# Splitting VectorE's copy of the gates' input parts in a two-group recurrence

## The reference

```
xi, xg, xo = xt @ U_i + b_i, xt @ U_c + b_c, xt @ U_o + b_o
def step(carry, xs):
    h, c = carry
    i_t = sigmoid(xi_t + h @ V_i)
    g_t = tanh(xg_t + h @ V_c)
    o_t = sigmoid(xo_t + h @ V_o)
    c_new = h * c + i_t * g_t
    h_new = o_t * tanh(c_new)
    return (h_new, c_new), h_new
```

## Time and profile before

| | |
|---|---|
| median of 3 runs | 3816.36 us (3816.0 to 3819.65) |
| the profiled execution | 3818.34 us, span 3816.5 us |
| busy share of the span | PE 92%, PEld 77%, DVE 76%, ACT 64%, POOL 34% |
| granted clock of TensorE, mean | 0.978 |
| VectorE copies into psGI (L2147) | 192, median 684 ns |
| GpSimd hc (L2205) | 192, mean 735 ns |

### The profile page before, as it was taken

How to read it: one execution, slowest core, us unless ns; L and a number is a source line. 1 busy time by engine, 2 the same in 40 slices (tenths; PEclk the granted TensorE clock), 3 DMA queues, 4 the chain that set the end, 5 groups by cost and what they waited for, 6 DMA issues and landing times. The chain is left out here.

```text
span 3816.5 us, 81795 instructions
## 1 busy us (share of the span) xinstructions
PE 3493.4 (92%) x30707; PEld 2953.6 (77%) x30707; DVE 2918.6 (76%) x4371; ACT 2444.4 (64%) x6220; POOL 1309.3 (34%) x735
## 2 busy tenths in 40 slices
PE   8878888888879988999999989999999979899987
PEld 7755555555559977888888878888888878788886
DVE  4679999999968865777777766777777767677887
ACT  4548888888855545666666655666666633677775
POOL 0009999999955541000000001000000024222254
PEclk9989999999989989999999999999999989999999
DMA  5674111211124321000000010000000046555575
GB/s 147 196 207 108 44 39 44 64 41 44 39 69 135 118 93 46 18 18 17 18 18 12 12 53 17 18 18 17 18 18 12 12 153 211 170 144 143 143 227 166
DMA packets 199348, 294.39 MB, mean 77 GB/s; under 512 B 17920, under 2 KB 155520, under 8 KB 195968
## 3 DMA queue, kind: packets, MB, share of 16 engines
q1 hardware_dynamic: 189824, 282.08, 24.7%
q10 hardware_dynamic: 9216, 8.39, 0.6%
HBM read 197.87 MB, written 92.54 MB: 76 GB/s over the span
## 5 line engine op out<-in xcount | busy, mean ns | idle before, releaser
L737 POOL TENSOR_TENSOR mx_big<-mp_lvs,mx_big 128x1280 f32<-128x1280 f32 (+1 forms) x224 | 709.9, 3239 | 282.3 <-ACT mp_lvs L657 277.5
L712 DVE TENSOR_TENSOR mx_big<-mp_psL,mx_big 128x2816 f32<-128x2816 f32 (+1 forms) x224 | 691.4, 3145 | 21.2 <-PE mp_psO L602 18.3
L664 ACT ACTIVATE mp_cut<-mp_psO,mx_mask 128x128 f32<-128x128 f32 x2048 | 553.1, 405 | 140.1 <-PE mp_psO L602 110.2
L602 PE MATMUL mp_psO<-mx_big,mp_pair 128*16 128x256 f32 x8192 | 498.5, 383 | 110.8 <-DVE mx_big L712 84.9
L1538 PE MATMUL sv_psO<-at_v_hi,sv_p_hi 128*128 128x258 f32 x2048 | 584.0, 285 | 13.5 <-DVE sv_p_lo L1626 10.3
L1557 ACT ACTIVATE sv_S<-sv_psS,at_kb 128x512 f32<-128x512 f32 x512 | 353.0, 689 | 372.1 <-PE sv_psS L1512 294.3
L1538 PE MATMUL sv_psO<-at_v_lo,sv_p_hi 128*128 128x258 f32 x2048 | 578.6, 282 | 0.0
L1538 PE MATMUL sv_psO<-at_v_hi,sv_p_lo 128*128 128x258 f32 x2048 | 577.7, 282 | 0.0
L1601 DVE TENSOR_TENSOR sv_run<-sv_run,sv_S 128x512 f32<-128x512 f32 x448 | 313.3, 699 | 289.2 <-ACT sv_S L1557 289.2
L602 PEld LDWEIGHTS mp_psO<-mx_big,mp_pair 128*16 128x16 f32 x8192 | 324.7, 127 | 249.2 <-DVE mx_big L712 136.9
L1538 PEld LDWEIGHTS sv_psO<-at_v_hi,sv_p_hi 128*128 128x128 f32 x2048 | 386.2, 189 | 43.1 <-DVE sv_p_lo L1626 21.1
(11 more groups left out here) (288 smaller groups left out, 7724.1 us busy)
## 6 DMA issues: line engine op xcount, KB each, us to landing
re_xg<-xg SPq DMA_DIRECT2D x192, 384.0 KB, 3.3
xg<-ga_xg SPq DMA_DIRECT2D x32, 768.0 KB, 4.0
att<-mx_big SPq DMA_DIRECT2D x16, 1024.0 KB, 6.7
mp_pair<-att SPq DMA_DIRECT2D x128, 128.0 KB, 2.9
mx_big<-rv SPq DMA_DIRECT2D x14, 1024.0 KB, 11.9
fr_xr<-in_x SPq DMA_DIRECT2D x16, 512.0 KB, 4.7
fr_xl<-in_x SPq DMA_DIRECT2D x32, 256.0 KB, 4.2
rv<-fr_rvs SPq DMA_DIRECT2D x16, 512.0 KB, 3.2
```

What stands on the lines that cost most here:

```text
L602: mm = pe.matmul(psO[32 * j:32 * j + 2 * H, c % 2, q, :], pair[:, s, :, :, c * YC + y], Z[:, c % 2, y, :], start=True, stop=True, tile_pos ...
L664: ins = nc.scalar.activation(cut[:, s, c, :, h * DK:(h + 1) * DK], psO[:, c % 2, :, h * DK:(h + 1) * DK], ACT.Copy, scale=mask[:, h:h + 1])
L712: nc.vector.tensor_tensor(Z[:, c % 2, 0:m], psL[:, s, 0:D].unsqueeze(1).broadcast_to([P, m, D]), rv_place(big, seventh, b, c)[:, 0:m], ALU ...
L737: nc.gpsimd.tensor_tensor(Z[:, c % 2, m:YC], lvs[:, s, :].unsqueeze(1).broadcast_to([P, YC - m, D]), rv_place(big, seventh, b, c)[:, m:YC] ...
```

## The change

The copy is made in two halves of 256 columns, each with its own semaphore. The half for gate g stays where the copy was, behind c and ahead of the wait for tanh. The half for gate i is made later in the same slot, behind ig and ahead of `keep_lo`. TensorE waits for the second half only before its matmuls on gate i; SyncE waits for both before it reloads the buffer. The first steps' copies, before the slots, are made in two halves one behind the other.

```diff
-        per_group = ("gi_filled o_filled ...
+        per_group = ("g_filled i_filled o_filled ...
@@ SyncE
-                            sp.wait_ge(q[g]["gi_filled"], r.nth(i - S) + 1)
+                            sp.wait_ge(q[g]["g_filled"], r.nth(i - S) + 1)
+                            sp.wait_ge(q[g]["i_filled"], r.nth(i - S) + 1)
@@ TensorE
                         pe.wait_ge(q[g]["hi_ready"], n + 1)
-                        pe.wait_ge(q[g]["gi_filled"], n + 1)
+                        pe.wait_ge(q[g]["g_filled"], n + 1)
                         terms(g, psGI[g][:, 1, 0:D], G_, HI)
+                        pe.wait_ge(q[g]["i_filled"], n + 1)
                         terms(g, psGI[g][:, 0, 0:D], I_, HI)
@@ VectorE, in cell
                         if i + 1 < r.steps:
-                            fill_gi(g, i + 1)
+                            fill_g(g, i + 1)
                         dve.wait_ge(q[g]["tanh_ready"], n + 1)
@@
-                    def fill_gi(g, i):
+                    def fill_g(g, i):
                         dve.wait_ge(xg_in[g][i % S], r.load(i))
                         reach(dve, q[g]["g_ready"], r.nth(i))
+                        nc.vector.tensor_copy(psGI[g][:, 1, 0:D], xg[:, g, i % S, G_]).then_inc(q[g]["g_filled"], 1)
+
+                    def fill_i(g, i):
                         reach(dve, q[g]["i_ready"], r.nth(i))
-                        gates = xg[:, g, i % S].rearrange("p (j d) -> p j d", j=3)
-                        nc.vector.tensor_copy(psGI[g][:, :, 0:D], gates[:, 0:2]).then_inc(q[g]["gi_filled"], 1)
+                        nc.vector.tensor_copy(psGI[g][:, 0, 0:D], xg[:, g, i % S, I_]).then_inc(q[g]["i_filled"], 1)
@@
                     for g in range(B):
-                        fill_gi(g, 0)
+                        fill_g(g, 0)
+                        fill_i(g, 0)
@@ VectorE, the slots
                         nc.vector.tensor_tensor(ig[:, g], gate[:, g, I_], gate[:, g, G_], ALU.mult).then_inc(q[g]["ig_ready"], 1)
+                        if 0 <= m < r.steps - 1:
+                            fill_i(o, m + 1)
                         if k < r.steps:
                             keep_lo(o, k)
```

More of the change, by code:

```diff
@@ L1925, in recurrent_steps @@
         outed = [[sem(f"outed{g}{s}") for s in range(S)] for g in range(B)]
-        per_group = ("gi_filled o_filled turned moved hi_ready lo_ready g_made i_made o_made g_ready i_ready o_ready ig_ready c_ready "
+        per_group = ("g_filled i_filled o_filled turned moved hi_ready lo_ready g_made i_made o_made g_ready i_ready o_ready ig_ready c_ready "
                      "tanh_ready h_ready hc_ready os_ready").split()
```

## The result

The changed kernel takes 3850.5 us (median of 4 runs) against 3816.2 us before: ratio 1.009, 95% interval 1.0076 to 1.0104. It is 34 us slower, as forecast (3851, with 34.0 us in the sum). The profiled execution took 3849.08 us, with a span of 3847.3 us.

A forecast was written before the change was run, and what follows sets the result against it. It took VectorE's own queue order (h_lo of one group, then c of the other) to bound the kernel at 2.77 us a slot. Terms 28.2 + 5.8 gave +34.0 us, so 3851 us, range 3824 to 3866.

The forecast's parts named there:

- (b) to (d): VectorE, fill_i between ig and h_lo: 0.33 us, slots of 2.99; +28.2 us in the first 128, +5.8 in the last 64.
- The price of the half: VectorE's 256-column copy behind ig: taken as 0.33 us a slot, between bounds of 0.20 and 0.60.
- The sum: Whole recurrence: 28.2 + 5.8 = +34.0 us.
- Part (a): Copy between c and h shrinks to 256 columns, so h waits only for tanh: gain 0.03 us a slot.
- What bounds the kernel before: Recurrence slot: a loop closed once a slot on VectorE's queue order, h_lo of one group, then c of the other: 2.77 us.
- The link from h to the cast: From h through the transposes to the cast at +1.08, which ends at +1.47 and releases h_lo at +1.50.
- The page's chain through TensorE: Profile page's chain, mostly through TensorE: not followed, because TensorE sits idle twice in every slot, once for 0.24 us.
- rival C: VectorE: fill_i fits before the cast, only the 0.03 gain is left: -6 us, 3810; chance 0.04.
- rival A: VectorE: ig is not really held by hc, only slowed by chance: total +7 us, 3823; chance 0.06.
- B: Last 64 slots: fill_i too is held by GpSimd, at the residual add: total +69 us, 3885; chance 0.08.
- Part (e): New waits, TensorE for the I half before its fifth gate matmul and SyncE's one more per load: costed at nothing.
- the cover: TensorE's margin from fill_i's end at +1.84 to its fifth gate matmul at +2.09: 0.25 us.

The follow-up runs named there:

- experiment 7: Changed kernel with a second copy of the same 256 columns ahead of fill_i, behind ig, into unused columns of the bank: 3916.5 us.
- experiment 1: Changed kernel with the half for gate i right behind h, ahead of ig, instead of behind ig: 3815.3 us, ratio 0.9998.
- experiment 9: Changed kernel with gate i's half behind h, ig written to PSUM, and the cast ahead of the o copy on ScalarE: 3791.8 us.
- experiment 5: Kernel before with only the cast h_hi moved ahead of the o copy in ScalarE's queue: 3808.4 us, ratio 0.9978.
- experiment 10: Changed kernel with gate i's half behind h, gate i left in PSUM, and the cast ahead of the o copy: 3785.2 us.
- experiment 4: Changed kernel with ScalarE's sigmoid of gate i left in PSUM, so ig has one SBUF and one PSUM input: 3811.2 us.
- Experiment 2: Kernel before with the whole 512-column copy moved, unsplit, from the cell to behind ig: 3956.9 us, ratio 1.0371.

## Why the prediction came out right, and where it read the trace wrongly

- **The new slot, (b) to (d): right.** 1.42 + 0.33 + 0.34 + 0.90 = 2.99 was forecast, 1.44 + 0.33 + 0.33 + 0.90 = 3.00 measured, in both parts. The price of the half, chosen between 0.20 and 0.60, is 0.33 by the trace and by experiment 7. The prediction's estimate of 0.42 us for a half, from the Trainium skill ("VectorE: DVE Perf Modes", the section on the TRN2 errata), agrees with the recorded 0.41; the page gives its formula for the fp32 add of two tensors, and the copy comes out near it too.
- **The sum: right, and a little small.** From 2.77 to 3.00 in 128 slots is 29 us, from 2.90 to 3.00 in 64 is 6 us, and the recurrence grew by 35.3; the sum had 34.0.
- **Part (a), the gain of 0.03: the mechanism is right, h follows tanh by 0.03.** It is part of the new slot's 0.90. Taken alone in the first 128 slots it is worth nothing: experiment 1 has it and its slot there is 2.77. In experiment 9, with ScalarE's loop shortened, it counts: 2.67 against 2.69 in experiment 5.
- **What bounds the kernel before: wrong.** The step that fails is "I don't follow that chain", with the sentence that the loop "is closed once a slot, on VectorE's own queue order". The sum 1.50 + 0.34 + 0.93 = 2.77 holds for any sequence of rows that repeats with the slot; it does not show that each link waited for the one before it. The link from h to the cast did not: the cast waited for ScalarE's queue, and had 0.12 to 0.14 us of slack (+1.08 against +0.94 to +0.96). The page's chain through TensorE was nearer to the truth, though it left out ScalarE's share; TensorE's own work is not the limit at 2.77, since it fits into the 2.60 of experiment 10. Experiment 5 decides this: 8 us came from a place in ScalarE's queue to which the prediction's reading gave no value.
- **Why the total survived.** The slot before was measured, and the slot after runs through hc, ig and h_lo, a route that was read rightly. So the error in the loop of before did no harm to the sum. It entered the price of rival C (-6 us), which experiment 1 corrects to no measurable change, and that of rival A (+7 us): with ig not held, experiment 4 has 3811.2 us, 4 us below before. The hold is thus worth some 37 us in the changed kernel, and not the 27 between forecast and rival A.
- **Rivals.** A falls: ig ends 0.28 after hc in each row shown, and experiment 4 shows what an ig that isn't held does. The trace agrees with the Trainium skill's rule ("SBUF — State Buffer", "Who interferes with whom"): the product with two SBUF inputs is blocked (0.83 us), that with one SBUF and one PSUM input is not (0.42). B falls by experiment 4 and by the changed kernel, whose fill_i takes 0.41 in the last slots too.
- **Part (e): the cost of nothing is right, the cover is not.** TensorE's first gate matmul moved up to +1.47 with the earlier cast, so the fifth starts at +1.96 and not +2.09; fill_i ends at +1.85. That leaves 0.11 of the 0.25, and a matmul's weight load starts ahead of it: the load is 0.06 late in each slot. So TensorE does wait for fill_i, which the prediction had named as a sign of being wrong. It costs nothing here: ig starts at +0.69, earlier than the +0.77 forecast, and its end is set by hc, 0.28 after it. In experiment 7 this load is some 0.39 late, and the slot still grows only by 0.32. Experiment 2 shows the price when the first matmul has to wait.
- **What the page shows after.** The page's chain of the changed kernel runs from c through tanh and both gates to ig, not through h and hc, since a gate ended ig's idle time. But ig's end follows hc, and in experiment 4, where the gates still come ahead of ig and only the hold is gone, the slot falls from 3.00 to 2.78.

## What to carry to other kernels

An instruction that is moved "behind" another in an in-order queue is also moved ahead of everything that follows there. Look for the place where that engine waits anyway: here that is between h and ig, where the half costs nothing; one instruction later, behind ig, it costs 34 us. And a loop of rows whose times add up to the period proves nothing by itself; ask at each link whether the instruction started because of the one before it, or because its own engine's queue let it go only then.

## What the runs showed of the hardware

- The hold between VectorE and GpSimd goes both ways. The residual add took 0.91 to 0.92 us when ig (two SBUF inputs) was waiting as hc ended, and 0.74 when ig had one input in PSUM; ig in turn ended 0.28 after hc.
- The same product took 0.83 us from SBUF in the changed kernel and 0.42 with one input in PSUM, under the same GpSimd instruction. Keeping one operand in PSUM took the changed kernel's ratio from 1.009 to 0.9992, some 37 us.
- VectorE's copies of 256 columns from SBUF to PSUM start 0.33 us apart and take 0.41 to 0.42; the copy of 512 columns takes 0.69 and lets the next start after 0.60. Two halves cost 0.06 us more of the queue than the whole.
